# One copy ahead of a third exponential, one low part ahead of a third maximum: an order edit in a fused FFN, attention, FFN kernel

## The reference

```python
x = x + 0.5 * ffn(layernorm(x))       # SwiGLU form: (silu(x Wu^T) * (x Wg^T)) Wd^T, ternary weights, hidden 1024
x = x + attn(layernorm(x))            # causal softmax attention, 16 query heads and 4 key/value heads of 16
x = x + 0.5 * ffn(layernorm(x))
```

## Time and profile before

| | |
|---|---|
| median of 3 runs | 591.67 us (591.05 to 592.29) |
| the profiled execution | 591.82 us, of it the span of the trace 590.1 us |
| granted TensorE clock | 0.997 of full speed |
| busy share of the span | PE 95%, PEld 58%, DVE 81%, ACT 68%, POOL 29% |
| busy in 230 to 400 us (170 us) | PE 163.80, PEld 105.85, DVE 155.26, ACT 141.63, POOL 90.94 |
| first projection of a chunk starts at | 214.71, 242.91, 270.11, 298.31, 325.51, 353.71 us |

### The profile page before, as it was taken

How to read it: one execution, slowest core, us unless ns; L and a number is a source line. 1 busy time by engine, 2 the same in 40 slices (tenths; PEclk the granted TensorE clock), 3 DMA queues, 4 the chain that set the end, 5 groups by cost and what they waited for, 6 DMA issues and landing times.

```text
span 590.1 us, 12391 instructions
## 1 busy us (share of the span) xinstructions
PE 558.4 (95%) x4244; PEld 344.3 (58%) x4244; DVE 479.8 (81%) x1861; ACT 400.3 (68%) x717; POOL 170.2 (29%) x264
## 2 busy tenths in 40 slices
PE   2889999999999989999999999997999999999998
PEld 2346565555666755666666656554455565566566
DVE  6898978989875889898989897995797688756654
ACT  5857665674655368798888888886666665674642
POOL 3115201101530035454546463665401101100100
PEclk9999999999999999999999999998999999999999
DMA  8711101100105151423323323212201212111112
GB/s 313 223 26 37 21 19 34 36 19 19 37 18 126 40 112 57 94 81 69 95 57 102 84 66 84 68 49 38 37 1 36 72 40 69 37 55 54 36 37 72
DMA packets 72222, 37.90 MB, mean 64 GB/s; under 512 B 35520, under 2 KB 71616, under 8 KB 72128
## 3 DMA queue, kind: packets, MB, share of 16 engines
q1 hardware_dynamic: 72160, 37.11, 24.3%
HBM read 18.22 MB, written 10.49 MB: 49 GB/s over the span
## 4 chain that ended last, share of the span: by engine, by line
PE 73%; DVE 18%; ACT 3%; issue 2%; POOL 2%; DMA 2%; SPq 1%; DVEq 0%; POOLq 0%; ACTq 0%
PE bank L1167 33%; PE bank L1179 17%; DVE sm_out L984 7%; PE bank L1266 5%; PE bank L1323 4%; PE bank L1334 4%; PE bank L1293 4%; PE bank L1339 2%; PE bank L1348 2%; PE bank L1143 1%; DVE hid L853 1%; DVE stats L733 1%; POOL xn L413 1%; DVE hl L868 1%; DVE q_hl L972 1%
## 5 line engine op out<-in xcount | busy, mean ns | idle before, releaser
L984 DVE CUSTOM_DVE_ANT_0 sm_out<-bank,mask 128x256 f16<-128x256 f32 (+1 forms) x512 | 151.3, 352 | 16.9 <-PE bank L1293 16.1
L486 ACT ACTIVATE silu<-bank,w_scale 128x512 f32<-128x512 f32 x128 | 87.5, 684 | 112.9 <-PE bank L1167 112.9
L853 DVE SCALAR_TENSOR_TENSOR hid<-silu,h_unit,bank 128x512 f32<-128x512 f32 x128 | 95.0, 743 | 63.8 <-ACT silu L486 63.5
L1179 PE MATMUL bank<-wT_down,hh 128*128 128x256 f16 x512 | 118.3, 273 | 2.5 <-DVE hl L868 2.3
L1179 PE MATMUL bank<-wT_down,hl 128*128 128x256 f16 x512 | 118.2, 273 | 0.0
L1167 PE MATMUL bank<-xh,wT_up 128*128 128x512 f16 x256 | 98.0, 383 | 1.0 <-DVE xl L797 0.7
L868 DVE TENSOR_TENSOR hl<-hid,hh 128x512 f16<-128x512 f32 x128 | 98.6, 770 | 0.0
L1167 PE MATMUL bank<-xh,wT_gate 128*128 128x512 f16 x256 | 97.0, 379 | 1.6 <-DVE hid L853 1.6
L1167 PE MATMUL bank<-xl,wT_up 128*128 128x512 f16 x256 | 98.0, 383 | 0.0
L1167 PE MATMUL bank<-xl,wT_gate 128*128 128x512 f16 x256 | 97.0, 379 | 0.0
L422 POOL TENSOR_TENSOR xnl<-xn,xnh 128x1024 f16<-128x1024 f32 x13 | 28.3, 2179 | 213.2 <-ACT xn L525 177.8
(11 more groups left out here) (134 smaller groups left out, 791.7 us busy)
## 6 DMA issues: line engine op xcount, KB each, us to landing
q_st<-q_scratch SPq DMA_DIRECT2D x32, 256.0 KB
q_scratch<-q_hl SPq DMA_DIRECT2D x16, 256.0 KB, 2.2
out_dram<-x SPq DMA_DIRECT2D x7, 512.0 KB, 3.0
x<-in_x_dram SPq DMA_DIRECT2D x1, 3072.0 KB, 15.5
k_scratch<-k_hl SPq DMA_DIRECT2D x16, 128.0 KB, 2.4
k_st<-k_scratch SPq DMA_DIRECT2D x16, 128.0 KB
x<-in_x_dram SPq DMA_DIRECT2D x2, 512.0 KB, 4.4
shared<-in_w_up_t_dram SPq DMA_DIRECT2D x2, 512.0 KB, 6.7
```

The lines of the kernel that those rows point to most:

```text
L486: act.activation(silu[:, e % 2, :], U[e % 2][:, :], ACT.Silu, scale=w_scale[:, 0:1]).then_inc(silu_ready, 1)
L853: dve.scalar_tensor_tensor(out=hid[:, e % 4, :], in0=silu[:, e % 2, :], scalar=h_unit[:, 0:1], in1=GT[e % 2][:, :], op0=ALU.mult, op1=ALU. ...
L984: ins = dve.tensor_tensor_reduce(sm_out[:, i, cols], SM[i][:, cols], mask[:, S - size:S], -1.0 / MAX_UNIT, -MASKED, ALU.add, ALU.min, rowm ...
L1179: ins = pe.matmul(ACC[t % 2][:, 0:D], part[:, par, e, t * P:(t + 1) * P], wT_down[:, e, :], start=(e == 0 and part is hh), stop=(e == NE - ...
```

## The change

Two operations change their place in the order of their engine; none is added, removed or altered. ScalarE, at even k, g = 0 (not in the last pair): `xT_copy` of the first half goes ahead of the third exponential of the group. VectorE, at odd k, g = 1 (not in the last pair): `query_low` of the second query part goes ahead of the third maximum. Each happens six times.

```diff
                         if not (end and g == 3):
-                            exps(n + 1, range(1, 3))
+                            exps(n + 1, range(1, 2))
                         if not odd and g == 0 and not last:
                             xT_copy(c + 2, range(0, 1))
+                        if not (end and g == 3):
+                            exps(n + 1, range(2, 3))
                         if end and g == 3:
 
                             act.activation(hid[:, 3, 0:1], ones[:, 0:1], ACT.Silu)
...
-                            if odd and g == 1 and i == 2 and not last:
+                            if odd and g == 1 and i == 1 and not last:
                                 query_low(c + 2, 1)
```

## The result

The changed kernel took 585.66 us (median of 5 runs, 585.36 to 586.84), the kernel before 591.05 beside it. The ratio is 0.9908, with a 95% interval of 0.9895 to 0.9921: 5.4 us faster, where 4.3 were forecast. The base alone is enough for that: before had a median of 591.67 when I predicted and 591.05 now, 0.6 us less. Both kernels have executions with a granted TensorE clock of 1.000 and of 0.997 of full speed, about 1.3 us apart in span (before 588.5 to 589.5 and 589.7 to 590.5), and a median of five depends on how many of each it holds. The two profiled executions both had 0.997; their spans are 590.1 and 585.1, a difference of 5.0 us. I account for those 5.0 us.

The account below looks back on a forecast made before the run. TensorE was taken to hold most of the chain, so reordering pays only where it stands still. Terms 3.0 − 0.3 + 1.6 = 4.3 us took the 591.67 us median to 587.4 us, range 586.1 to 590.6.

Parts of the forecast that it names:

- A: Main forecast: both moves pay in the attention phase, 4.3 us faster, 587.4 us; chance 0.52.
- the weight load of the first projection: At the six xT places: given no term of its own beside the 3.0 us of stalls.
- VectorE's sum of work: At k = 1: unchanged until the next third maximum, so existing waits absorb most delay; cost 0.3 us, bounds 0 and 0.9.
- The step on the last pair: Last pair, no copy to wait for: TensorE's 0.47 us wait for the maxima goes, within the 1.6 us DMA gain.
- The stalls at the six places: TensorE's first projection waits for xT, 3.0 us in all; scores wait for the maxima's DMA at four places, 1.1 us.
- So the whole stall goes: At six places, k = 0 and 2: the early xT copy removes TensorE's whole wait before the first projection, 3.0 us.
- The chain now starts 1.4 or 0.75 us earlier, and each stall is less than that: SP's queue from scratch write to maxima copy: earlier q_hl removes the DMA waits; gain 1.6 us, bounds 0 and 2.4.
- Rival B: Only the copy's move pays; DMA engines' load sets the maxima's landing: 2.1 us faster, 589.6 us; chance 0.26.
- No cost to the third exponential: ScalarE at six places: the 0.59 us copy fits a 0.75 us gap, so the exponential starts as before.
- The two parts as terms of a sum: Both moves priced separately and added: 3.0 − 0.3 + 1.6 = 4.3 us.
- part 2: VectorE's query low part ahead of the third maximum, k = 1 and 3, g = 1: cost 0.3 us, gain 1.6 us.
- Rival E: Weight loads' idle time is the true stall: 3.7 + 2.4 (DMA waits) = 6.1 us faster, 585.6 us; chance 0.07.

Follow-up runs that it names:

- the fill: Changed kernel with GpSimd's causal masks replaced by fills of 1.0, so causal masking is left out: 582.16 us, ratio 0.9857.
- SP's order: SP's scratch reads put behind the copy of the second half's maxima: 584.85 us on the changed kernel, 586.32 us with only the xT copy moved.

## Why the prediction was wrong, and where right

At the places the mechanisms of A were there. The sum, 4.3 us, was 0.7 too small against the 5.0 of the two profiles. Two steps failed upwards: the weight load of the first projection was put at nothing (0.59 us), and VectorE's sum of work was called unchanged (0.3 us of cost that was 0.34 of gain). The step on the last pair failed the other way (0.47 us of gain that was 0.40 of loss) and hid a good part of this. The base, 0.6 us lower now, did as much again to bring the time out of the range. By its own steps:

- **The stalls at the six places: right, a little small.** Forecast 3.0 for the copy and 1.1 for the landing, 4.1; measured 4.36 together. For the sixth place I had taken the printed idle time, 0.38, where the starts gave 0.54.
- **The weight load of the first projection: missing.** "So the whole stall goes" counted from start to start of the projection. Here the matmul's weight load waited for the same copy, and it is hidden once it needn't wait: 0.1 us each, 0.59 in all. It goes with the copy's wait and not with the DMA's: with the copy alone the distance to the second projection is 0.87 us even at places that still wait for the landing, and with the low part alone it is 0.98.
- **"VectorE's sum of work until then is unchanged": failed.** Cost 0.3 forecast, a gain of 0.34 measured, so 0.64 of the error. The change puts the 0.75 us low part under GpSimd's two masks, where two of the short steps stood. In the kernel before at k = 1:

```profile
286.66 0.64 POOL L365 TENSOR_SCALAR_AFFINE_SELECT shared<-shared 128x512 f32<-128x512 f32 x1 [1.61 <-ACT shared L596]
286.93 0.38 DVE L767 SCALAR_TENSOR_TENSOR newton<-newton,rstd 128x8 f32<-128x8 f32 x1
...
287.25 0.64 POOL L368 TENSOR_SCALAR_AFFINE_SELECT shared<-shared 128x512 f32<-128x512 f32 x1
...
287.65 0.25 DVE L769 SCALAR_TENSOR_TENSOR rstd<-newton,rstd 128x8 f32<-128x8 f32 x1
```

  and in the changed one:

```profile
284.07 0.64 POOL L365 TENSOR_SCALAR_AFFINE_SELECT shared<-shared 128x512 f32<-128x512 f32 x1 [1.62 <-ACT shared L596]
...
284.13 0.74 DVE L974 SCALAR_TENSOR_TENSOR q_hl<-bank,b_col,q_hl 128x512 f16<-128x512 f32 x1
...
284.66 0.64 POOL L368 TENSOR_SCALAR_AFFINE_SELECT shared<-shared 128x512 f32<-128x512 f32 x1
...
285.00 0.31 DVE L769 SCALAR_TENSOR_TENSOR newton<-newton,rstd 128x8 f32<-128x8 f32 x1
...
285.66 0.15 DVE L771 SCALAR_TENSOR_TENSOR rstd<-newton,rstd 128x8 f32<-128x8 f32 x1
```

  Each long step ends where the mask ends, to 0.02 us: 286.93 + 0.38 and 286.66 + 0.64, 287.65 + 0.25 and 287.25 + 0.64, 285.00 + 0.31 and 284.66 + 0.64. The low part, with one of its inputs in PSUM, takes the same time under the masks as without. The two steps take 0.46 instead of 0.63 us, and that is the 0.16 by which the stretch is shorter. In the first stretch another step meets a mask in the changed kernel and takes 0.64 us, at 228.25, which uses up the gain: 0.02. The Trainium skill has this rule, and I had not used it: "SBUF — State Buffer", section "SBUF: two separate sides", says that a VectorE operation with two SBUF inputs and a GpSimd operation that reads SBUF take a shared pair of ports as an exclusive lock, for the whole instruction. The runs agree, with the mask and with the fill, which reads nothing: 0.31 and 0.16 us for the same step, at 285.00 in the changed kernel and at 283.26 with fills. But the held step's row ends with the mask's and not a step's 0.16 us behind it, which the traces don't explain. The part about TensorE was right: 0.80 us of wait at 232.69, taken back at the next third maximum.
- **"In the last pair it is 0.47 us" as a gain: failed.** From the sixth place's end on, the kernel lost 0.49 us by the compared matmul, 0.40 by the end of the span. "The chain now starts 1.4 or 0.75 us earlier, and each stall is less than that" took it that the landing moves with the write's issue. Here it didn't: the early write took 3.41 us to its reads instead of 2.17, and the wait grew to 1.16. But the copy of `xT` alone loses as much in this pair without an early write, so the write explains only that first wait. What sets these landings stays open; SP's order removes the waits. Rival B's sign, a write closer behind the copies, was there at all three k = 3 places, and the late landing at one; that the DMA engines' load is the reason is not shown.
- **No cost to the third exponential: right**, and it would have been small without the gap.
- **The two parts as terms of a sum: right in the total, wrong as prices.** I had the DMA's 1.1 us at the places as part 2's gain. Alone, part 2 gives 0.3 us, because the projection starts behind the later of two things.

The sum: 4.36 + 0.59 + 0.34 − 0.40 + 0.10 (a difference ahead of the first place that the change has no part in) = 5.0 us; the −0.40 is what the others leave of the spans' difference. With −0.49 it gives the 4.9 us at the matmul.

Rival E named the measured time, 585.6, by luck: its gain was 6.1 us from the higher base, against 5.4 measured. Its first term was near, though: the weight loads' idle time of 3.7 us is stall and load together, and 3.0 + 0.59 is what these came to. Its second, 2.4 us from the DMA waits, was not there. Printed idle time gave 2.0 us for the copy and the starts 3.0. The Trainium skill's sentence that the prediction drew on for this ("Perfetto Trace Analysis", section "Identifying the Most-Contended Engine") has pipelined matmuls look smaller in a trace; here a row is longer than the time to the next start, 0.38 against 0.22 us, so idle time looks smaller.

## What to carry to other kernels

Look under GpSimd's operations before you call VectorE's sum of work unchanged: a short step with both inputs in SBUF that started under a mask took until the mask's end. When one instruction waits for two things, removing either wait alone is worth only what the other leaves: here 2.9 and 0.3 us alone, 4.9 together. Read the stall from start to start, and add the weight load if it waits for the same thing. A DMA whose data is ready but which stands behind a wait and four transfers on its queue is a cheaper thing to mend than the work that this wait is for: one line of SP's order gave all of it and the last pair too.

## What the runs showed of the hardware

A step of VectorE on 128 x 8 fp32 with two inputs in SBUF takes 0.16 us, and up to 0.64 us when it starts while a GpSimd mask of 128 x 512 runs that reads SBUF. The 27 such steps, of which some meet a mask, cost 7.4 us in the changed kernel, 5.1 moved to other places of the order, and 4.5 beside fills. A low part that reads PSUM and one SBUF tensor took 0.74 us under the masks and 0.75 without.

A write of 256 KB to DRAM took mostly 2.2 us (2.4 and 2.6 at two places) to the first read behind it when issued about 0.9 us after two small copies, and at one place 2.7 to 3.4 us when issued directly behind them, at others 2.3 to 2.4.
